# Four fused cross-attention layers: the third attention moved behind the next pair's first, value lanes spread by copies through memory, and an order of steps for each engine

## The chip, the cores and the metric

One core of one Trainium2 chip. The time is that of the whole launch on the device, in microseconds (us). The engines are TensorE (matrix products; PE in the profile, PEld for its weight loads), VectorE (DVE), ScalarE (ACT), GpSimd (POOL) and SyncE (SP), which here issues every DMA.

## What is computed

Sixteen sequences of 128 tokens and 256 channels pass through four layers, each with the same context `ctx`. All data is float32.

```python
# layer 0: 16 heads of 16; x attends to ctx and to itself; then RMSNorm and an MLP with GELU
# layer 1: 32 query heads, 8 key heads of 8; x attends to ctx; then LayerNorm
# layer 2: a recurrence over the tokens, 32 heads of 8, with the state from ctx
def step(s, inp):
    k_l, v_l, w_l, r_l = inp
    a = k_l[..., :, None] * v_l[..., None, :]
    out = jnp.einsum('bhs,bhst->bht', r_l, faaaa * a + s)
    s_new = a + w_l[..., None] * s
    return (s_new, out)
# r, k, v, g, w are projections of five mixtures of a token with the one before it;
# the result is normalised by head, gated by g, projected; then a gated feed-forward step
# layer 3: 16 heads of 16; x attends to LayerNorm(ctx); hidden + tanh(gate) * out @ Wo.T
```

## The kernel before

A **turn** works on a pair of sequences (`PAIR` = 2), so there are eight. A turn's work is cut into named **steps**, in three streams: entry (transposes `xT`, `cT` and the first queries, keys, values), front (layers 0 and 1, and layer 3's keys `k3` and values `v3`), and back (layers 2 and 3). Streams of different pairs run in one phase: `start` holds entry of pair 0; `first` front of 0 and entry of 1; each of six `steady` phases back of i, front of i+1, entry of i+2; `closing` back of 6 and front of 7; `last` back of 7.

**Order.** `SCHEDULE` is one hand-written list of steps for a steady phase. Every engine goes through the same list (`steps_of`) and does its own part of each step; each engine's queue is strict, and engines meet only at semaphores. `FIRST_ORDER` and `LAST_ORDER` serve the ends.

**Attention** runs in jobs (`("job", layer, n)`, 16, 16 and 8 a turn for layers 0, 1, 3). Job n multiplies scores for jobs n and n+1 (TensorE, line 534), masks them and finds the maximum (VectorE, L1020), exponentiates (ScalarE, L831), transposes (L548), copies out of PSUM (VectorE, L1035) and weighs values into the accumulator `psO` (L579, L587) with some steps' delay. `psO` is shared: attention 0, then the gathers of layer 2 (`y`), then attention 1, then attention 3 use it, each waiting until the one before is read.

**Products.** Other matrix results go through three PSUM banks (`ring`); a step's `start` waits until the product three before it has left. A product with two output tiles and two input tiles is 8 records of TensorE in the trace (L494, L504), a transpose step 4 (L485), m2 32 (L504 with hT).

**The lane steps** of layer 2 deal with the state s (8 by 8 a head) as 8 pairs u of lanes, with the token axis in the free dimension. For each u, `vr{u}` spreads v over the lanes by two products with a 0/1 matrix (`spread_v`, L599), VectorE multiplies the result in PSUM with k into `kv` (L1233), GpSimd puts the initial state in front (`seed`, L1381), VectorE runs two scans along the tokens (L1240) into `SS`, GpSimd multiplies by r into `Z` (L1371), and `gather` (odd v only, L614) sums lanes on TensorE into `psO`. `y` = psO + bonus (L1248). `kv` and `SS` are rings of two, `Z` of four. r is `rT`, v is `vT`, copied out of the product v2 at L1205; `ruk` is L1210, `g2` L1215, `bonus` L1220.

**Values.** `values16` (L1063, L1066) and `v1` (L1157) lay each value head beside zeros with 4 narrow instructions a product, so that 32-wide weight loads put a head in its rows.

`cT` is L1109, norms are L984 to L996, `o0` L1139, `m2` L1149, `o3` L1295. SP waits before each transfer for the reader of the old content; its order in a phase is mask and initial state of the back, mask 1, context, x and mask 0 of the entry, output.

## Time and profile before

| | |
|---|---|
| runs of the kernel before | 1258.09, 1263.58, 1264.42 us; median 1263.58 |
| profiled execution | 1264.44 us, of which span 1262.5 |
| TensorE (PE) busy | 1127.0 us, 89% |
| VectorE (DVE) | 956.6 us, 76% |
| ScalarE (ACT) | 651.5 us, 52% |
| GpSimd (POOL) | 261.0 us, 21% |
| mean granted TensorE clock | 0.945 of 2.4 GHz |
| moved by DMA | 18.91 MB, mean 15 GB/s |

The span runs from the first to the last instruction. Busy time of TensorE covers records whose ends are modelled; records of one kind overlap a little, so a group's busy time is less than count times mean. "Idle before" a group is time in which its engine stood still just before one of its instructions, with the engine that released it.

### The profile page before, as it was taken

To read this page: it belongs to the slowest core of one execution; us is meant where nothing else is said; L and a number is where in the kernel's file an instruction comes from. 1 tells how busy PE (TensorE), PEld (TensorE's weight loads), DVE (VectorE), ACT (ScalarE), POOL (GpSimd) and SP (SyncE) were. 2 spreads that over 40 slices of the span, in tenths; PEclk is the share of its full clock that TensorE was granted. 3 is DMA by queue.
4 is the path that set the end of the run, shared out by engine and by line. 5 is a ranking of instruction groups with operands and counts; after the bars stand their busy time and mean duration, and the time that the engine had idled before them with its cause. 6 is when DMAs were issued, how large, how long until landed. Compare 5 with 4: busy or idle time off the path is not lost. (4 is left out here: it accounts for less than half of the span.)

```text
span 1262.5 us, 24184 instructions
## 1 busy us (share of the span) xinstructions
PE 1127.0 (89%) x7776; PEld 765.1 (61%) x7776; DVE 956.6 (76%) x3401; ACT 651.5 (52%) x2483; POOL 261.0 (21%) x349
## 2 busy tenths in 40 slices
PE   5878899999999998999999998999999998897656
PEld 4564666665665666666666666666666666554434
DVE  2707697789967998789968998689968998675834
ACT  1528343784448553774448553674438553582024
POOL 3210223102410214102420214102321214101310
PEclk9788899999999999999999999999999999898858
DMA  8000000000000000000000000000000000000000
GB/s 296 2 9 20 1 2 1 22 2 15 2 21 2 16 1 1 22 2 16 1 22 2 12 5 1 22 2 15 1 22 2 6 11 1 1 2 11 1 1 9
DMA packets 18092, 18.91 MB, mean 15 GB/s; under 512 B 7216, under 2 KB 16432, under 8 KB 17712
## 3 DMA queue, kind: packets, MB, share of 16 engines
q1 hardware_dynamic: 17968, 17.37, 4.6%
q8 instruction: 64, 1.05, 0.3%
q14 instruction: 60, 0.49, 0.1%
HBM read 15.27 MB, written 2.10 MB: 14 GB/s over the span
## 5 line engine op out<-in xcount | busy, mean ns | idle before, releaser
L831 ACT ACTIVATE E<-S,nmax 128x128 f32<-128x128 f32 (+1 forms) x1024 | 424.1, 416 | 229.4 <-DVE nmax L1020 215.1
L1020 DVE CUSTOM_DVE_ANT_0 S<-psS,mb 128x128 f32<-128x128 f32 (+1 forms) x1024 | 264.3, 320 | 87.7 <-PE psS L534 64.4
L494 PE MATMUL ring<-slot,w_l 128*128 128x256 f32 x992 | 251.5, 400 | 14.0 <-DVE slot L1202 5.2
L494 PEld LDWEIGHTS ring<-slot,w_l 128*128 128x128 f32 x992 | 188.8, 198 | 60.0 <-issue 12.8
L548 PEld LDWEIGHTS psT<-ident,E 128*128 128x128 f32 x1280 | 146.2, 147 | 128.1 <-ACT E L831 73.3
L534 PE MATMUL psS<-keys,slot 32*128 32x512 f32 (+1 forms) x768 | 194.4, 581 | 30.1 <-DVE nmax L1020 19.0
L1035 DVE COPY ET<-psT 128x512 f32<-128x512 f32 x320 | 206.2, 681 | 7.8 <-PE psT L548 7.8
L548 PE MATMUL psT<-ident,E 128*128 128x128 f32 x1280 | 203.8, 293 | 7.8 <-DVE ET L1035 3.2
L831 ACT ACTIVATION_READ_ACCUMULATOR E<-S,nmax 128x1 f32 x1024 | 191.6, 187 | 0.0
L504 PE MATMUL ring<-w_l,slot 128*128 128x256 f32 (+1 forms) x640 | 151.9, 384 | 7.7 <-DVE slot L1051 5.8
L504 PEld LDWEIGHTS ring<-w_l,slot 128*128 128x128 f32 x640 | 115.3, 194 | 36.6 <-issue 10.7
L534 PEld LDWEIGHTS psS<-keys,slot 32*128 32x128 f32 x768 | 65.7, 190 | 78.6 <-DVE nmax L1020 37.7
L1240 DVE TENSOR_TENSOR_SCAN SS<-wP,kv 128x258 f32<-128x258 f32 x128 | 104.3, 854 | 2.2
L485 PE MATMUL ring<-ident,slot 128*128 128x128 f32 x384 | 61.0, 291 | 47.3 <-ACT slot L868 19.0
L1020 DVE DVE_READ_ACCUMULATOR2_ANT nmax<- 128x1 f32 x1024 | 84.7, 83 | 0.0
L485 PEld LDWEIGHTS ring<-ident,slot 128*128 128x128 f32 x384 | 46.3, 147 | 63.2 <-ACT slot L868 22.6
L1371 POOL TENSOR_TENSOR Z<-SS,slot 128x512 f32<-128x512 f32 x64 | 76.8, 1200 | 26.9 <-DVE SS L1240 26.9
L804 ACT ACTIVATE slot<-ring 128x512 f32<-128x512 f32 x72 | 42.5, 591 | 68.0 <-PE ring L485 55.3
L1389 POOL TENSOR_SCALAR veps<-mv 128x2 f32<-128x2 f32 x32 | 7.0, 218 | 314.0 <-DVE mv L989 314.0
L599 PE MATMUL ring<-slot,spread 128*128 128x256 f32 x256 | 70.2, 401 | 0.3
L815 ACT ACTIVATE hT<-ring,colt 128x256 f32<-128x256 f32 x64 | 26.9, 471 | 82.2 <-PE ring L494 82.2
L579 PE MATMUL psO<-ET,V 128*32 128x128 f32 x1536 | 63.2, 283 | 1.3 <-DVE ET L1035 1.3
(119 smaller groups left out, 1183.3 us busy)
## 6 DMA issues: line engine op xcount, KB each, us to landing
slot<-in_ctx SPq DMA_DIRECT2D x8, 256.0 KB, 2.7
slot<-in_x SPq DMA_DIRECT2D x8, 256.0 KB, 2.7
w_l<-in_wl SPq DMA_DIRECT2D x1, 2048.0 KB, 11.2
out<-slot SPq DMA_DIRECT2D x8, 256.0 KB, 2.1
w_l<-in_wl SPq DMA_DIRECT2D x2, 768.0 KB, 7.1
w_l<-in_wl SPq DMA_DIRECT2D x1, 1152.0 KB, 9.9
m0i<-in_m SPq DMA_DIRECT2D x8, 128.0 KB, 3.2
mb<-in_m SPq DMA_DIRECT2D x8, 128.0 KB, 2.8
```

What stands on the lines that cost most here:

```text
L485: m = pe.transpose(b[:, c, a * P:(a + 1) * P], src[:, a, c * P:(c + 1) * P], ident[:, :])
L494: m = pe.matmul(b[:, a, :], w[:, k, m0 + a * P:m0 + (a + 1) * P], src[:, k, :], start=(k == 0), stop=(k == kt - 1))
L504: m = pe.matmul(b[:, bb, 0:n], src[:, k, bb * P:(bb + 1) * P], w[:, k, :], start=(k == 0), stop=(k == kt - 1))
L534: ins = pe.matmul(psS[(first_job[layer] + m) % 2][:, x * w:(x + 1) * w], queries, keys[rows, group % RING_K, x * w:(x + 1) * w], start=Tru ...
L548: m = pe.transpose(psT[g % 2][:, k, :], E[:, g % RING_E, k * P:(k + 1) * P], ident[:, :])
L579: m = pe.matmul(psO[32 * c:32 * c + 32, t, bb * P:(bb + 1) * P], v[:, t * P + 32 * c:t * P + 32 * c + 32], e, start=(half == 0 and sblk == ...
L599: m = pe.matmul(b[:, a, :], spread_j[:, j + a, :], vT[:, ct, :], start=True, stop=True)
L831: ins = act.activation(E[:, g % RING_E, h * w:(h + 1) * w], S[:, g % RING_S, h * w:(h + 1) * w], ACT.Exp, bias=nmax[:, g % 4, h:h + 1], sc ...
L1020: ins = dve.tensor_tensor_reduce(S[:, g % RING_S, h * w:(h + 1) * w], psS[g % 2][:, h * w:(h + 1) * w], bias[:, bb, :], -1.0, HUGE, ALU.ad ...
L1035: dve.tensor_copy(ET[:, g % 4, :, :], psT[g % 2][:, :, :]).then_inc(sems["copied"], 1)
L1240: ins = dve.tensor_tensor_scan(SS[:, u % 2, a, :, :].rearrange("p b t -> p (b t)"), wP[:, ct, :, :].rearrange("p b t -> p (b t)"), kv[:, u ...
L1371: pool.tensor_tensor(Z[:, v % 4, :, :].rearrange("p a (b t) -> p a b t", b=PAIR), SS[:, v % 2, :, :, 0:P], r, ALU.mult).then_inc(sems["z"], 1)
```

## The change

Layer 3's attention (`job 3`, `inv3`, `sum3`, `o3`) becomes a fourth stream, one phase later: it now runs between attention 0 and the lane steps of the *next* pair, and `psO` is used in the order attention 0, attention 3, `y`, attention 1. `k3` and `v3` go from the front to the back stream. There are seven phases (`start`, `first`, `second`, five `steady`, `closing`, `last`, `end`), and the output and X4 get slots of their own (23, 24).

The spread products are gone. SP writes each half of `vT` to a buffer in memory, every row eight times, waits for each write, and reads it back in the lane layout, one transfer for each lane pair into a ring of four (`VR`). The multiplication with k moves from VectorE to GpSimd, which reads `VR`.

Values are written with one instruction a product; a weight load takes a `window` of 32 columns so that the head falls at its place.

Each engine has its own order (`PE_ORDER`, `ACT_ORDER`, `DVE_ORDER`, `POOL_ORDER`), written out for every phase; `@phase` names the phase of the words behind it, so that steps of two phases mix. In it `j3.6-7` are jobs 6 and 7 of layer 3. The quoted lines are one steady turn. Waits now count by these orders.

```diff
+def window(head, place, d):
+
+    at = 32 * head + 32 - d - d * place
+    return slice(at, at + 32)
...
+RING_V = 4
...
-SCHEDULE = [
-    "mask0", "xaT", *jobs(0, 0, 2), "shift1", *jobs(0, 2, 3), "cols", *jobs(0, 3, 4), "t", *jobs(0, 4, 8), "mw",
...
+PE_ORDER = """
...
+j1.8 v0l j1.9-11 o2 j1.12-13 k1 j1.14 xcT j1.15 @steady1 j0.0 @steady0 j1.16-17 fr j1.18 fk @steady1 j0.2 @steady0
+sum1 j1.19 @steady1 j0.3-4 @steady0 fv @steady1 j0.5-7 @steady0 o1 @steady1 j0.8-9 @steady0 x4T v1 @steady1 j0.10-11
+@steady0 q3 @steady1 j0.12-15 xaT j3.0 j0.16 k3 j0.17 j3.2 sum0 j3.3 j0.19 j3.4-5 o0 t j3.6-7 mw nT j3.8 mk mv j3.9 d1
+mr d2 v2 k2 j3.11 sum3 r2 o3 mg bonus u0 g2 u1 u2 u3 v3 gather1 m2 gather3 aT gather5 x1T q1 gather7 cT j1.0 yT xT
+j1.2 q0 j1.3 k0l ynT j1.4 k0c j1.5-7 v0c j1.8-9 v0l j1.10-11 o2 j1.12-13 k1 j1.14 xcT j1.15 @steady2 j0.0 @steady1
+j1.16-17 fr j1.18 fk @steady2 j0.2 @steady1 sum1 j1.19 @steady2 j0.3-4 @steady1 fv @steady2 j0.5-7 @steady1 o1
+@steady2 j0.8-9 @steady1 x4T v1 @steady2 j0.10-11 @steady1 q3 @steady2 j0.12-15 xaT j3.0 j0.16 k3 j0.17 j3.2 sum0 j3.3
+j0.19 j3.4-5 o0 t j3.6-7 mw nT j3.8 mk mv j3.9 d1 mr d2 v2 k2 j3.11 sum3 r2 o3 mg bonus u0 g2 u1 u2 u3 v3 gather1 m2
+gather3 aT gather5 x1T q1 gather7 cT j1.0 yT xT j1.2 q0 j1.3 k0l k0c j1.4 v0c j1.5-7 ynT j1.8 v0l j1.9-11 o2 j1.12-13
...
+ACT_ORDER = """
...
+@steady1 j0.3-9 @steady0 x4T @steady1 j0.10-11 @steady0 q3 @steady1 j0.12-15 xaT j3.0 k3 j3.1-2 sum0 j3.3-5 hn t
+apply0 j3.6-7 d1 d2 decay k2 sum3 r2 u0 g2 u1 u2 u3 aT x1T yT xT j1.0-1 yn k0l j1.2-4 ynT j1.5 k0c j1.6-13 k1 xcT
+j1.14-15 @steady2 j0.0-1 @steady1 fr fk @steady2 j0.2 @steady1 sum1 @steady2 j0.3-9 @steady1 x4T @steady2 j0.10-11
...
+DVE_ORDER = """
...
+cols j0.15 j3.0 j0.17 inv0 j3.2-3 shift1 sum0 j3.4-5 o0 j3.6-7 mw nT inv3 mk mv mr j3.9 v2 sum3 ruk o3 mg bonus vr0
+vr1 g2 vr2 vr3 v3 vr4 vr5 vr6 m2 vr7 q1 yT cT @steady2 norm3 @steady1 j1.0 @steady2 mask0 @steady1 yn j1.2-3 q0
+@steady2 apply3 @steady1 j1.4-5 y2 j1.6-7 v0c j1.8-9 v0l j1.10-11 o2 norm4 j1.12-13 apply4 j1.14-15 shift0 j1.17
+@steady2 j0.0 @steady1 inv1 @steady2 j0.2-3 @steady1 sum1 @steady2 j0.4-5 @steady1 fv @steady2 j0.6-7 @steady1 o1
...
+POOL_ORDER = """
...
+@steady0 norm1 @steady1 j0.12 @steady0 apply1 @steady1 sum0 @steady0 norm2 @steady1 j3.0 j3.4 hn j1.0 vr0 vr1 vr2
+gather0 vr3 gather1 vr4 gather2 vr5 gather3 vr6 gather4 vr7 gather5 gather6 gather7 x1T @steady2 norm3 @steady1 norm4
+@steady2 j0.0 j0.4 j0.8 @steady1 norm1 @steady2 j0.12 @steady1 apply1 @steady2 sum0 @steady1 norm2 @steady2 j3.0 j3.4
...
+FINAL = {"inv3", "sum3", "o3"}
...
+HAS = {"start": (0,), "first": (0, 1), "second": (0, 1, 2), "steady": (0, 1, 2, 3), "closing": (1, 2, 3), "last": (2, 3),
+       "end": (3,)}
+TIMES = {"start": 1, "first": 1, "second": 1, "steady": TURNS - 3, "closing": 1, "last": 1, "end": 1}
...
+IN_ORDER = {"start": [], "first": [0, 1], "second": [0, 1], "steady": [0, 3, 1], "closing": [0, 3, 1], "last": [3], "end": [3]}
...
-        spread_j = sb("spread", [8, P])
+        VR = sb("VR", [RING_V, 2, T])
+        v_rows = nc.dram_tensor("v_rows", (P, 8, CT * T), F32, kind="Internal").ap()
+        v_spread = v_rows.rearrange("(c a h) i n -> c a (h i) n", c=4, a=2)
...
+        slot = [sb(f"slot{n}", [512]) for n in range(1, 25)]
...
-        rT, X3, OUT = cm(18), tm(18), tm(18)
+        rT, X3, OUT = cm(18), tm(18), tm(23)
         kT, kk = cm(19), cm(19)
-        vT, tmpv, X4 = cm(20), tm(20), tm(20)
+        vT, tmpv, X4 = cm(20), tm(20), tm(24)
         gT, x4T = cm(21), cm(21)
         shifted = sb("shifted", [CT, PAIR, P + 1])
         wP = sb("wP", [CT, PAIR, P + 1])
...
+        V0 = sb("V0", [2, PAIR, 16 * 32 + 16])
+        V1 = sb("V1", [PAIR, 8 * 32 + 24])
+        V3 = sb("V3", [PAIR, 16 * 32 + 16])
...
+                final = {"steady": loop, "closing": TURNS - 3, "last": TURNS - 2, "end": TURNS - 1}.get(phase)
...
+                if back is not None:
+                    sp.wait_ge(leaves("v2"), left("v2"))
+                    for ct in range(CT):
+                        half = slice(ct * T, (ct + 1) * T)
+                        sp.dma_start(v_rows[:, :, half], vT[:, ct, :].unsqueeze(1).to_broadcast([P, 8, T]))\
+                            .then_inc(sems[f"v_out{ct}"], 16)
+                    for u in range(8):
+                        ct, j = u // 4, 2 * (u % 4)
+                        half = slice(ct * T, (ct + 1) * T)
+                        if j == 0:
+                            sp.wait_ge(sems[f"v_out{ct}"], turn(f"v_out{ct}"))
+                        if u >= RING_V:
+                            sp.wait_ge(sems["kv"], turn("kv", u - RING_V + 1))
+                        sp.dma_start(VR[:, u % RING_V, :, :],
+                                     v_spread[j % 4:j % 4 + 2, j // 4, :, half].rearrange("c p t -> p c t"))\
+                            .then_inc(sems[f"v_in{u % RING_V}"], 16)
+                if final is not None:
+                    sp.wait_ge(leaves("o3"), left("o3"))
+                    sp.dma_start(out[final], OUT).then_inc(sems["out_done"], 16)
+                if entry is not None:
                     if phase != "start":
                         sp.wait_ge(leaves("aT"), left("aT"))
-                    sp.dma_start(CX, ctx_in[shift:][entry]).then_inc(sems["c_in"], 16)
+                    sp.dma_start(CX, ctx_in[entry]).then_inc(sems["c_in"], 16)
...
-                        pe.wait_ge(sems["attn3"], before("attn3"))
+                        pe.wait_ge(sems["attn1"], before("attn1"))
+                    if layer == 3 and n == 0:
+                        if phase == "last":
+                            pe.wait_ge(sems["attn1"], before("attn1"))
+                        elif phase == "end":
+                            pe.wait_ge(sems["y"], before("y"))
+                        else:
+                            pe.wait_ge(sems["attn0"], turn("attn0"))
...
-                def spread_v(u):
-
-                    ct, j = u // 4, 2 * (u % 4)
-                    b = start(f"vr{u}")
-                    for a in range(2):
-                        m = pe.matmul(b[:, a, :], spread_j[:, j + a, :], vT[:, ct, :], start=True, stop=True)
-                    m.then_inc(sems["product"], 1)
...
-                    for half in range(2):
-                        for ct in range(CT):
-                            d = dst[:, :, half, ct * P:(ct + 1) * P]\
-                                .rearrange("p b (c h d) -> p b c h d", h=2, d=16)[:, :, :, half, :]
-                            at = ct * P + half * 64
-                            v = bank(phase, name)[:, :, at:at + 64].rearrange("p b (c d) -> p b c d", d=16)
-                            if name == "v3":
-                                ins = dve.tensor_copy(d, v)
-                            else:
-                                bias = row["v0_b"][:, at:at + 64].rearrange("p (c d) -> p c d", d=16)
-                                ins = dve.tensor_tensor(d, v, bias.unsqueeze(1).to_broadcast([P, PAIR, 4, 16]), ALU.add)
+                    d = dst[:, :, 16:].rearrange("p b (h x) -> p b h x", x=32)[:, :, :, 0:16]
+                    v = bank(phase, i, name).rearrange("p b (h d) -> p b h d", d=16)
+                    if name == "v3":
+                        ins = dve.tensor_copy(d, v)
+                    else:
+                        bias = row["v0_b"].rearrange("p (h d) -> p h d", d=16)
...
                             dve.wait_ge(sems["w"], turn("w"))
-                        dve.wait_ge(sems["product"], product(step))
-                        if u >= 2:
-                            dve.wait_ge(sems["scan"], turn("scan", u - 1))
                         dve.wait_ge(sems["seed"], turn("seed", u + 1))
-                        k_ = kT[:, ct, :].rearrange("p (b t) -> p b t", b=PAIR).unsqueeze(1)\
-                            .to_broadcast([P, 2, PAIR, P])
-                        dve.tensor_tensor(kv[:, u % 2, :, :, 1:P + 1],
-                                          bank(phase, step).rearrange("p a (b t) -> p a b t", b=PAIR), k_,
-                                          ALU.mult).then_inc(sems["emptied_D"], 1)
-                        dve.wait_ge(leaves(step), left(step))
...
+                        dve.wait_ge(sems["x4"], before("x4"))
+                        dve.wait_ge(sems["out_done"], before("out_done"))
...
+                def key_times_value(u):
+
+                    ct = u // 4
+                    pool.wait_ge(sems[f"v_in{u % RING_V}"], turn(f"v_in{u % RING_V}", 16 * (u // RING_V + 1)))
+                    k_ = kT[:, ct, :].rearrange("p (b t) -> p b t", b=PAIR).unsqueeze(1).to_broadcast([P, 2, PAIR, P])
+                    pool.tensor_tensor(kv[:, u % 2, :, :, 1:P + 1],
+                                       VR[:, u % RING_V, :, :].rearrange("p a (b t) -> p a b t", b=PAIR), k_,
+                                       ALU.mult).then_inc(sems["kv"], 1)
...
+                            pool.wait_ge(leaves("k2"), left("k2"))
                         seed(u)
+                        key_times_value(u)
...
```

## Rows read from the trace of the kernel before

**Rows 1.** Windows by phase. Columns: window, its length, busy us (records) of PE, PEld, DVE, ACT, POOL, PEclk, DMA share, GB/s

```profile
0.00:145.50 145.50, 115.92 (x696) 77.58 (x696) 70.75 (x310) 60.06 (x228) 26.96 (x42) 0.87 0.22 71
145.50:291.70 146.20, 138.79 (x978) 94.03 (x976) 118.90 (x425) 81.62 (x312) 31.61 (x41) 0.96 0.02 6
291.70:1008.50 716.80, 674.30 (x4862) 461.69 (x4860) 596.82 (x2116) 404.50 (x1551) 158.33 (x205) 0.99 0.03 9
1008.50:1149.70 141.20, 126.27 (x910) 83.61 (x908) 113.65 (x409) 77.90 (x304) 29.86 (x39) 0.96 0.02 4
1149.70:1262.50 112.80, 71.68 (x336) 48.17 (x336) 56.50 (x146) 27.43 (x91) 14.23 (x22) 0.72 0.02 6
```

**Rows 2.** Windows of one looped turn: v2's copy to `y`, and the rest

```profile
457.50:497.50 40.00, 36.09 (x264) 24.83 (x263) 37.86 (x77) 15.12 (x45) 16.13 (x22) 1.00 0.01 1
497.50:600.90 103.40, 98.81 (x712) 67.54 (x712) 81.68 (x348) 65.81 (x266) 15.47 (x20) 0.98 0.04 12
```

**Rows 3.** Windows of the last phase: to v2's copy, from there to `y`

```profile
1149.70:1173.10 23.40, 17.98 (x53) 11.07 (x54) 9.37 (x20) 3.22 (x8) 0.00 (x0) 0.64 0.06 14
1173.10:1199.40 26.30, 16.69 (x85) 10.82 (x83) 22.87 (x30) 1.80 (x4) 10.92 (x16) 0.88 0.00 1
```

**Rows 4.** Groups of TensorE: line, operation, shapes, count, busy us, mean ns, idle before

```profile
L599 PE MATMUL ring<-slot,spread 128*128 128x256 f32 x256 | 70.2, 401 | 0.3
...
L485 PE MATMUL ring<-ident,slot 128*128 128x128 f32 x384 | 61.0, 291 | 47.3 <-ACT slot L868 19.0 <-DMA slot<-in_ctx 10.2 <-DVE slot L996 7.4
L504 PE MATMUL ring<-w_l,hT 128*128 128x256 f32 x256 | 57.4, 382 | 1.2 <-ACT hT L815 0.9
...
L614 PE MATMUL psO<-Z,gather 128*32 128x256 f32 x256 | 21.5, 409 | 8.9 <-POOL Z L1371 8.9
```

**Rows 5.** TensorE in order of time: start, length, line, operation; a looped turn, last phase

```profile
452.62 3.72 PE L494 MATMUL ring<-slot,w_l 128*128 128x256 f32 x16 [0.74 <-DVE slot L1202]
...
457.28 1.13 PE L534 MATMUL psS<-keys,slot 32*128 32x512 f32 x4
458.34 1.09 PE L548 MATMUL psT<-ident,E 128*128 128x128 f32 x8
459.36 0.65 PE L579 MATMUL psO<-ET,V 128*32 128x128 f32 x16
...
1163.98 3.78 PE L494 MATMUL ring<-slot,w_l 128*128 128x256 f32 x8
```

**Rows 6.** Groups of VectorE: scans, key times value, one of the value copies

```profile
L1240 DVE TENSOR_TENSOR_SCAN SS<-wP,kv 128x258 f32<-128x258 f32 x128 | 104.3, 854 | 2.2
L1233 DVE TENSOR_TENSOR kv<-ring,slot 128x512 f32<-128x512 f32 x64 | 43.0, 672 | 4.1 <-PE ring L599 4.0
L1066 DVE TENSOR_TENSOR V<-ring,rowt 128x128 f32<-128x128 f32 x64 | 13.8, 279 | 13.7 <-PE ring L504 13.7
```

**Rows 7.** VectorE and GpSimd in order of time, two lane pairs of the last phase

```profile
1177.30 1.28 DVE L1240 TENSOR_TENSOR_SCAN SS<-wP,kv 128x258 f32<-128x258 f32 x2
...
1178.82 1.18 POOL L1371 TENSOR_TENSOR Z<-SS,slot 128x512 f32<-128x512 f32 x1
...
1181.21 0.21 POOL L1381 TENSOR_TENSOR kv<-s,wP 128x4 f32<-128x4 f32 x1 [1.21 <-DVE SS L1240]
1181.37 1.18 POOL L1371 TENSOR_TENSOR Z<-SS,slot 128x512 f32<-128x512 f32 x1
...
1181.75 1.93 DVE L1240 TENSOR_TENSOR_SCAN SS<-wP,kv 128x258 f32<-128x258 f32 x2
```

**Rows 8.** DMA: queue with packets, MB, share of 16 engines; issues with us to landing

```profile
q1 hardware_dynamic: 17968, 17.37, 4.6%
...
slot<-in_ctx SPq DMA_DIRECT2D x8, 256.0 KB, 2.7
...
w_l<-in_wl SPq DMA_DIRECT2D x1, 2048.0 KB, 11.2
out<-slot SPq DMA_DIRECT2D x8, 256.0 KB, 2.1
```

461 lines of the change are left out of this document (249 added, 212 removed).

## The prediction

> **What bounds the kernel now.** I read the busy time by phase first. Of the six looped turns the last five take 716.8 us, 143.4 each; there TensorE is busy 94% of the time (674.3 us), VectorE 83% and GpSimd 22% [rows 1]. The ends are looser: the last phase has TensorE busy 71.7 of 112.8 us at a mean clock of 0.72 [rows 1]. Next, one looped turn, from 457.5 to 600.9, cut at two places: the copy of v2 out of PSUM (457.5) and the end of `y`, the sum behind the last gather (497.5). Those 40.0 us hold 3.9 us of TensorE idleness, the other 103.4 us hold 4.6; VectorE has 2.1 us free in the 40.0, and 103.4 - 81.7 = 21.7 us outside [rows 2]. So TensorE's own work sets the length of a turn nearly everywhere, and the lane steps (vr0 to vr7 with the gathers) are the place where VectorE does. In the last phase the same steps take 26.3 us with VectorE busy 22.9 and TensorE only 16.7 [rows 3].
>
> **What the change takes away.** The eight spread products of a turn: 70.2 us of TensorE in the kernel [rows 4], 8.8 us a turn, so TensorE's busy time in a looped turn falls from 134.9 [rows 2] to 126.1. In the last phase TensorE is idle beside them, so there they give nothing. VectorE loses the key-times-value multiplication, 43.0 us, 5.4 a turn [rows 6]. The narrow value copies: 16 a turn at 0.22 us net (13.8/64) [rows 6] become three wide ones at the 0.67 of L1233 and one narrow, 3.5 to 2.2 us. VectorE's 119.5 us a turn become 112.8, less what its scans now wait for GpSimd (13.0 us a turn [rows 6] against eight pairs at 1.28 [rows 7]), so 110.0.
>
> **What it adds: the lane chain.** From v2's copy to `y` the path becomes: two writes of 1 MB to memory (each lane row eight times), a read of 256 KB per lane pair, then per pair a seed, the multiplication (now GpSimd), two scans (VectorE) and the Z product (GpSimd).
> The copies. 17,968 packets took 4.6% of 16 engines' span, 52 ns each [rows 8]. The writes are 2048 packets of 1 KB: 6.6 us. The first read is issued when the first write has landed, behind the second write in one queue: another 0.8 us for its 256 packets. A 256 KB write lands in 2.1 us and a read in 2.7 [rows 8], so some 1.9 us of a landing is not packets. 6.6 + 0.8 + 1.9, and 0.2 for issue: 9.5 us to the first multiplication. Bounds: 4.8 us (2.1 + 2.7, if size cost nothing) and 14 us (11.2, the landing of the 2 MB load, + 2.7) [rows 8]. I take 9.5, since packet time is the same everywhere in the trace. The other reads (0.8 us each) stay ahead of the steps.
> The steps. In the last phase Z starts at 1181.37 and takes 1.18 us; the scans start at 1181.75 and take 1.93 us, where two of them take 1.28 when alone [rows 7]: a scan waits for GpSimd to end. The mean scan takes 0.85 for the 0.64 of one alone [rows 6, 7]. The seed is 0.21 [rows 7]. Multiplication: not in the trace on GpSimd; Z has the same shape and number of inputs, 1.18. If one waits for the other throughout, a pair takes 0.21 + 1.18 + 1.18 + 1.28 = 3.85, less about 0.1 because a waiting scan ends a little sooner (1.93 against 0.80 + 1.28 = 2.08): 3.75, against 2.55 now (two Z starts at 1178.82 and 1181.37 [rows 7]). Bounds: 2.6 (GpSimd alone, nothing waits) and 3.9. Eight pairs: 30 us, 21 to 31.
> The Trainium skill's "SBUF — State Buffer", section "SBUF: two separate sides", says that GpSimd and a VectorE instruction with two SBUF inputs exclude each other for the whole instruction; the multiplication that this change moves had a PSUM input and was outside of that rule. By it alone a pair would be 3.89 and the sum 9 us longer than by the 3.75; the rows agree with it but for that 0.1.
> Chain from the end of v2 on TensorE to the end of the last gather: 0.7 (copy) + 9.5 + 30 + 0.65 (gather) + 0.4 of signals = 41.3 us.
>
> **What covers it.** In the new order of TensorE, from v2 to gather7 of a looped turn stand ten products of 8 records (k2, r2, o3, g2, u0 to u3, v3, q1) at 1.86 us (3.72/2 [rows 5]) = 18.6; m2 7.2 (57.4/8 [rows 4]); mg and bonus 1.0 each; sum3, aT, x1T 0.6 each (61.0 us for 96 [rows 4]); four gathers 2.7 (21.5/8 [rows 4]); one weighing step 0.65 [rows 5]. Sum 33. TensorE's queue is strict: it stands at gather5 and gather7, with layer 1's attention behind them, for 41.3 - 33 = 8.3 us, where it now loses 3.9.
> A looped turn: 41.3 + (126.1 - 33 = 93.1) + 4.6 (idle elsewhere, as now) = 139.0, 4.4 less than now. Five: -22.
> Second turn (now the first looped one, 146.2 [rows 1]): -8.8 spread; -13.3 for attention 3, which isn't there yet (four pairs of jobs at 2.7 us, from 457.28 to 459.98 [rows 5], = 10.8, sum3 0.6, o3 1.9); 34 us of cover, so 7 us of waiting for 3.9: +3. Together -19.
> Closing: -8.8, +4.4 for the wait, +13.3 for the attention 3 that comes from an earlier turn: +9.
> Last phase: the chain from v2's copy to `y` is 41.5 for 26.3 [rows 3]: +15. The attention of the turn before it (13.3) runs in front, where TensorE has idle 5.4 of 23.4 us at clock 0.64 [rows 3], and closing has 14.9 idle [rows 1]: I take 10 of the 13.3 as filled gaps (bounds 0 and 13.3): -10.
> First turn: k3 and v3 leave it (2 x 1.86, into the idle last phase): -4; its tail overlaps the next turn's jobs: TensorE is idle 29.6 us to 145.5 [rows 1], of which I take 4 (0 to 12).
> Small ones: the wait for the output's landing moves from ScalarE's r2 to VectorE's o3, a turn after that transfer: 0. SP's new waits (v2, then the ring of four) stand in front of the output and of the next CX and X. The ring is free some 26 us after v2, CX is wanted at cT, behind gather7 at 41; X waits for GpSimd's xb1, which stands behind the last Z, and comes near to when xT wants it: 0, at most 1 us a turn. The new slots and V tiles: 0.
> Sum against the profiled execution (span 1262.5, time 1264.4): 1264.4 - 22 - 19 + 9 + 15 - 10 - 4 - 4 = 1229.4, and the median of the runs is 0.9 below that execution. Forecast 1229.
>
> **Rivals.**
> (a) The chain is covered: scans and GpSimd run beside each other at 2.6 a pair, or the copies land in 5 us, or both in part. Then a looped turn is 126.1 + 4.6 = 130.7: five 41 us less than forecast, second 7, closing 8, last 9: 1164. For it: GpSimd is busy 31.7 of 143.4 us [rows 1]. Against it: the pattern of rows 7 repeats for every pair.
> (b) The clock. In the last phase, after waits, a product takes 3.78 us where it takes 1.86 in a looped turn [rows 5], and that stretch was granted 0.64 [rows 3]: the 1.2 GHz level for most of it. The looped turns are granted 0.99 [rows 1]; TensorE would now wait some 6 us at gather5 in each. Two products' worth at 1.2 GHz in seven turns: 2 x 1.9 x 7 = +27: 1256. The Trainium skill's "TensorE: Matmul & The Clock Gate", "Part 1: The HAM clock gate", says the same: throttled is the resting state and activity lifts it. Against: the wait at gather7 would absorb part of the slow stretch.
> (c) Slower: VectorE becomes the bound. It stands still in the chain for 41.3 - 17.6 us (16 scans 10.2, nine other steps 7.4), so 92.4 us of its work fall to the 97.7 us outside: 5 us of room where it has 21.7 now [rows 2]. Where its queue is in a stretch the later one (masks and copies of attention 1, token shifts, norms), TensorE waits for scores to be masked, and a turn is 146: +7 in seven turns, 1278. It decides once chain and VectorE's waits together cost 4.3 us a turn over the forecast (35 us over eight turns), that is, from a chain of 45.6 us, or copies of 14.
> (d) That the spread products were free already. In the 40.0 us they share TensorE is busy 36.1 [rows 2], so at most part of them; this lies inside (c).
>
> **How the numbers follow.** Forecast case 0.44 (own range 1205 to 1250), (a) 0.24 including halfway cases from 1160 to 1200, (b) 0.12, (c) 0.20. The range must leave out no more than 0.2: its low end 1172 cuts off about half of (a), its high end 1277 half of (c). A measurement of this kernel tells 0.5% (6.3 us) from no change. Faster by more: the forecast case, (a) and a third of (b): 0.70; within: 0.11; slower: 0.19.
>
> **What the changed profile would show.** TensorE busy near 1057 us and no line of spread products; GpSimd up by about 64 x 1.18 = 76 us, more if its records hold waiting. Looped turns of 139 us; TensorE's waits for Z grown from 8.9 us to some 50, in gather5 and gather7; scans with a mean well over 0.85 us; from v2's copy to the first multiplication 9 to 10 us; about 3.75 us from Z to Z; clock dips in every turn if (b). The prediction is wrong low if VectorE is busy or port-bound over 90% outside the chain, and wrong high if Z follows Z in 2.6 us.

## The result, and the profile after it

The changed kernel takes 1272.4 us (median of 17 runs, 1263.7 to 1281.9), the kernel before 1259.6 (17 runs beside them). The ratio of the runs is 1.0088, 95% interval 1.0058 to 1.0117 (that of the two medians is 1.010). Forecast were 1229 us, a range of 1172 to 1277 and, with 0.70, a faster kernel: the time lies near the upper end of the range, and the direction was wrong. The profiled execution of after is a long one: 1281.9 us, span 1280.0.

The page of after, the TensorE clock by fortieths of the span, and the groups that answer to [rows 4], [rows 6], [rows 7] and [rows 8]:

```profile
PE 1101.0 (86%) x7520; PEld 740.2 (58%) x7520; DVE 921.3 (72%) x3233; ACT 661.4 (52%) x2490; POOL 361.1 (28%) x413
...
PEclk9889796999999998999979999999999998689567
...
q1 hardware_dynamic: 52016, 50.93, 12.9%
...
L1326 DVE TENSOR_TENSOR_SCAN SS<-wP,kv 128x258 f32<-128x258 f32 x128 | 138.3, 1134 | 50.8 <-POOL Z L1463 44.1
...
L1481 POOL TENSOR_TENSOR kv<-VR,slot 128x512 f32<-128x512 f32 x64 | 92.1, 1440 | 20.5 <-DMA VR<-v_rows 20.5
...
L1463 POOL TENSOR_TENSOR Z<-SS,slot 128x512 f32<-128x512 f32 x64 | 85.6, 1339 | 15.0 <-DVE SS L1326 15.0
...
L723 PE MATMUL psO<-Z,gather 128*32 128x256 f32 x256 | 26.2, 496 | 50.2 <-POOL Z L1463 49.9
...
v_rows<-slot SPq DMA_DIRECT2D x16, 1024.0 KB, 6.5
VR<-v_rows SPq DMA_DIRECT2D x64, 256.0 KB, 3.7
```

TensorE waits 49.9 us for Z at the gathers (some 50 forecast, 8.9 before), the scans' mean is 1.13 us (forecast: well over 0.85). But TensorE is busy 1101 us where 1057 were forecast: the records are those expected, 256 fewer than before, and the granted clock is 0.917 for 0.945.

The windows of after, cut at the end of v2's copy of the first, the second, the seventh and the eighth turn (columns as in [rows 1]):

```profile
0.00:177.90 177.90, 148.94 (x981) 98.32 (x982) 102.07 (x391) 83.31 (x310) 34.52 (x52) 0.90 0.18 58
177.90:312.90 135.00, 121.16 (x826) 80.36 (x825) 106.59 (x375) 73.60 (x277) 42.52 (x46) 0.92 0.13 38
312.90:1042.20 729.30, 666.37 (x4752) 452.79 (x4751) 573.44 (x2034) 415.88 (x1577) 222.33 (x248) 0.96 0.12 38
1042.20:1174.50 132.30, 111.18 (x686) 72.52 (x685) 90.12 (x310) 64.41 (x247) 36.77 (x41) 0.86 0.12 35
1174.50:1280.00 105.50, 53.32 (x281) 36.17 (x279) 49.10 (x126) 24.19 (x82) 24.98 (x26) 0.69 0.15 45
```

The same cuts in the trace of before, and the cut used below for one of its turns (v2's copy to `y`, then the rest):

```profile
0.00:170.80 170.80, 138.81 (x840) 90.67 (x840) 91.09 (x379) 72.95 (x274) 29.97 (x46) 0.87 0.19 61
170.80:314.80 144.00, 136.47 (x974) 93.09 (x972) 119.62 (x423) 80.91 (x310) 31.62 (x41) 0.98 0.03 9
314.80:1031.40 716.60, 674.12 (x4862) 461.80 (x4860) 595.97 (x2115) 404.53 (x1550) 158.63 (x205) 0.99 0.03 9
1031.40:1173.80 142.40, 124.58 (x826) 83.00 (x825) 103.46 (x360) 68.90 (x266) 26.54 (x35) 0.92 0.01 3
1173.80:1262.50 88.70, 53.00 (x281) 36.50 (x279) 46.47 (x126) 24.21 (x83) 14.23 (x22) 0.74 0.01 4
```

```profile
458.20:496.80 38.60, 34.69 (x259) 24.13 (x258) 36.51 (x75) 14.64 (x44) 16.12 (x21) 1.00 0.01 1
496.80:601.60 104.80, 100.21 (x716) 68.22 (x716) 83.01 (x349) 66.28 (x267) 15.47 (x20) 0.98 0.04 12
```

Up to the second turn's v2 after is 1.9 us ahead (forecast 27), the five turns behind it cost 12.7 more (forecast 22 less), closing and end together 6.7 more (forecast 14). Against the forecast that is 25.1 us too long, 34.7 too long and 7.3 too short, 52.5 us in all.

One turn of after: v2's copy to `y`, and from there to the next v2's copy (columns as in [rows 2]; [rows 2] is the turn of before, with a cut at 457.5 that lies 0.7 ahead of the copy's end):

```profile
615.60:656.60 41.00, 34.20 (x177) 25.03 (x177) 24.91 (x30) 8.65 (x16) 25.06 (x25) 0.89 0.40 124
656.60:760.80 104.20, 97.97 (x742) 64.67 (x742) 86.46 (x368) 72.43 (x292) 19.71 (x24) 0.96 0.02 4
```

I call the first part the chain and the second the rest. In order of time, the chain of this turn:

```profile
624.94 1.27 POOL L1481 TENSOR_TENSOR kv<-VR,slot 128x512 f32<-128x512 f32 x1 [4.69 <-DMA VR<-v_rows]
...
629.28 1.70 POOL L1481 TENSOR_TENSOR kv<-VR,slot 128x512 f32<-128x512 f32 x1
...
630.94 1.18 POOL L1463 TENSOR_TENSOR Z<-SS,slot 128x512 f32<-128x512 f32 x1
...
633.46 1.57 POOL L1463 TENSOR_TENSOR Z<-SS,slot 128x512 f32<-128x512 f32 x1
...
648.74 1.08 PE L723 MATMUL psO<-Z,gather 128*32 128x256 f32 x8 [4.67 <-POOL Z L1463]
...
651.68 3.78 PE L612 MATMUL ring<-slot,w_l 128*128 128x256 f32 x8 [0.69 <-ACT slot L907]
```

And the granted clock around that gather (windows of TensorE alone: length, busy, PEclk, DMA share, GB/s):

```profile
644.00:646.00 2.00, 0.07 (x1) 1.00 0.00 0
646.00:648.00 2.00, 0.00 (x0) 0.89 0.44 131
648.00:650.00 2.00, 1.21 (x9) 0.50 0.00 0
...
654.00:656.00 2.00, 2.00 (x12) 0.50 0.33 101
656.00:658.00 2.00, 2.00 (x14) 0.55 0.30 95
658.00:660.00 2.00, 2.00 (x16) 1.00 0.00 0
```

The reader is to see three things. v2's copy ends at 615.6 and the first multiplication starts 9.4 us later: the copies are as forecast. The first Z starts 6.0 us behind that, after three multiplications. And gather5 waits 4.7 us, behind which the clock stands at 1.2 GHz for 9 us: a product of 8 records takes 3.78 us where it takes 1.86 at full clock [rows 5]. This is the mechanism of rival (b).

### The profile page after: what moved, and what is told of

Same layout as the page of the kernel before. It is cut to its first block, busy times and chain, and to the rows that moved or that the text cites. A ratio compares the mean times of both kernels' runs of the same rounds, so it can differ in the third digit from the quotient of the medians.

```text
span 1280.0 us, 23548 instructions
## 1 busy us (share of the span) xinstructions
PE 1101.0 (86%) x7520; PEld 740.2 (58%) x7520; DVE 921.3 (72%) x3233; ACT 661.4 (52%) x2490; POOL 361.1 (28%) x413
## 3 DMA queue, kind: packets, MB, share of 16 engines
q1 hardware_dynamic: 52016, 50.93, 12.9%
## 4 chain that ended last, share of the span: by engine, by line
PE 44%; DVE 14%; ACT 9%; POOL 7%; issue 6%; DMA 2%; DVEq 0%; POOLq 0%; ACTq 0%
PE ring L612 8%; PE ring L622 8%; PE psS L649 8%; PE psT L663 8%; ACT E L934 6%; DVE SS L1326 4%; POOL kv L1481 3%; PE ring L603 3%; POOL Z L1463 3%; PE psO L704 2%; DVE S L1114 2%; PE psO L696 2%; DVE ET L1129 2%; DMA VR<-v_rows 1%; DMA v_rows<-slot 1%
## 5 line engine op out<-in xcount | busy, mean ns | idle before, releaser
L612 PE MATMUL ring<-slot,w_l 128*128 128x256 f32 x992 | 259.6, 414 | 9.4 <-ACT slot L907 6.2
L612 PEld LDWEIGHTS ring<-slot,w_l 128*128 128x128 f32 x992 | 198.3, 207 | 55.0 <-issue 12.6
L1326 DVE TENSOR_TENSOR_SCAN SS<-wP,kv 128x258 f32<-128x258 f32 x128 | 138.3, 1134 | 50.8 <-POOL Z L1463 44.1
L622 PE MATMUL ring<-w_l,slot 128*128 128x256 f32 (+1 forms) x640 | 164.0, 405 | 9.0 <-DVE slot L1361 3.0
L622 PEld LDWEIGHTS ring<-w_l,slot 128*128 128x128 f32 x640 | 122.6, 207 | 37.5 <-issue 10.9
L603 PE MATMUL ring<-ident,slot 128*128 128x128 f32 x384 | 67.6, 307 | 40.0 <-DVE slot L1245 11.8
L1481 POOL TENSOR_TENSOR kv<-VR,slot 128x512 f32<-128x512 f32 x64 | 92.1, 1440 | 20.5 <-DMA VR<-v_rows 20.5
L1435 POOL TENSOR_TENSOR keys<-k0T,in 128x512 f32<-128x512 f32 x32 | 33.9, 1068 | 210.3 <-PE psS L649 205.0
L1463 POOL TENSOR_TENSOR Z<-SS,slot 128x512 f32<-128x512 f32 x64 | 85.6, 1339 | 15.0 <-DVE SS L1326 15.0
L603 PEld LDWEIGHTS ring<-ident,slot 128*128 128x128 f32 x384 | 47.4, 155 | 63.0 <-issue 23.1
L723 PE MATMUL psO<-Z,gather 128*32 128x256 f32 x256 | 26.2, 496 | 50.2 <-POOL Z L1463 49.9
```

The source lines that it names most:

```text
L603: m = pe.transpose(b[:, c, a * P:(a + 1) * P], src[:, a, c * P:(c + 1) * P], ident[:, :])
L612: m = pe.matmul(b[:, a, :], w[:, k, m0 + a * P:m0 + (a + 1) * P], src[:, k, :], start=(k == 0), stop=(k == kt - 1))
L622: m = pe.matmul(b[:, bb, 0:n], src[:, k, bb * P:(bb + 1) * P], w[:, k, :], start=(k == 0), stop=(k == kt - 1))
L1326: ins = dve.tensor_tensor_scan(SS[:, u % 2, a, :, :].rearrange("p b t -> p (b t)"), wP[:, ct, :, :].rearrange("p b t -> p (b t)"), kv[:, u ...
L1463: pool.tensor_tensor(Z[:, v % 4, :, :].rearrange("p a (b t) -> p a b t", b=PAIR), SS[:, v % 2, :, :, 0:P], r, ALU.mult).then_inc(sems["z"], 1)
L1481: pool.tensor_tensor(kv[:, u % 2, :, :, 1:P + 1], VR[:, u % RING_V, :, :].rearrange("p a (b t) -> p a b t", b=PAIR), k_, ALU.mult).then_in ...
```

## The experiments

A matmul of 128x256 counts as two records here, 0.465 us at full clock. Unless said otherwise a time is a median, measured beside the kernel before, whose median was 1258.8 to 1259.3 each time. One part of the change is in every kernel below and is nowhere tested alone: the values written with one instruction a product.

### Each half of the change alone

The third kernel puts the spread products back into the new orders:

```diff
-ORDER["POOL"] ... key_times_value(u)      (GpSimd, out of VR)
+ORDER["PE"] = with_spread(ORDER["PE"], ORDER["DVE"])   # vr0..vr7 as products of TensorE
+dve.tensor_tensor(kv[...], bank(phase, i, step), k_, ALU.mult)
```

> One part of the change alone: the new orders and the third attention behind the next turn's first, but the values spread by TensorE as before (eight spread products a turn, the key-times-value product on VectorE out of PSUM, no copies through memory; the spread products are put between the new order's products). By the terms of the forecast: second turn -13, closing +13, last phase -10, first turn -8: 18 us under the kernel before, 1242. TensorE busy near 1127 us and clock as before, 0.945. Rival (the new orders are what costs): 1265 or more, with TensorE's waits outside the lanes (E of ScalarE 25 us, nmax 19 us) as in the changed kernel.

It takes 1251.7 us, ratio 0.9955 (0.9927 to 0.9983), busy 1121 us, clock 0.957. The new orders are no cost; they are worth 7 us, less than half of the 18. TensorE's waits for E, 2.5 us before, are 23 here too.

The fourth does the reverse:

```diff
+PE_ORDER = ACT_ORDER = DVE_ORDER = POOL_ORDER = OLD_ORDER   # the schedule of the kernel before
-IN_ORDER = {..., "steady": [0, 3, 1], ...}
+IN_ORDER = {..., "steady": [3, 0, 1], ...}
```

> The other part alone: the values spread by copies through memory and the key-times-value product on GpSimd, but all four engines in the order of the kernel before, with the third attention in its old place. In that order v2 stands some 19 us ahead of vr0, so the 9.6 us of the copies are hidden; lane pairs come every 3.5 to 3.75 us where they came every 2.55. Theory: a looped turn loses 8.8 us of spread products and gains some 8 to 10 us of lanes with the 1.2 GHz stretch behind them, 143 to 147; the last phase is 10 to 15 us longer: 1270 to 1300. Rival (TensorE's 8.8 us a turn are the larger term, the lanes are hidden): 1215 to 1245.

1304.1 us, ratio 1.0349 (1.0322 to 1.0377), a looped turn 148.5. The copies and GpSimd's multiplication, alone, cost 45 us, though they take 70 us of work from TensorE. In the new orders the same exchange costs 21 us (1251.7 to 1272.4).

### Clock, copies and v2's place

The first kernel gives TensorE idle work in front of its waits:

```diff
+FILL = {"gather5": 16, "gather7": 8}
+pe.matmul(b[:, k // 2 % 2, :], W0["w1"][:, k % 2, 0:P], hT[:, k % 2, :], ...)   # n times, into the next bank
 gather_y(step[1])
```

> The changed kernel with idle work for TensorE: in front of gather5 16 matmuls and of gather7 8 matmuls (128x256, 0.23 us each at full clock) into the ring bank of the next product, which overwrites them; in the last phase 8, 24, 24 and 24 in front of the four gathers. Nothing else changes. Theory (the clock: the chain of lanes is as long as forecast, and what is lost to the forecast is TensorE at 1.2 GHz behind its waits at the gathers, busy time 1101 where 1057 was forecast): the 1.2 GHz stretches behind the gathers of the looped turns go, the looped turns shorten by 3 to 6 us each, the mean granted clock rises from 0.917 to over 0.94, and the time falls by 20 to 40 us, to 1235 to 1255. Rival (VectorE's and ScalarE's waits outside the chain set the turn): the clock rises all the same, the time stays within 5 us of the changed kernel's 1272. Second rival (the matmuls delay more than they give): slower than 1277.

1340.2 us. It was mis-sized: I had taken a matmul for one record, so 115 us were added, most of them longer than the wait. It only shows that the clock follows (0.943). The sized one:

```diff
+FILL = {("second", None, "gather3"): 6, ("steady", 1, "gather5"): 8, ("steady", 2, "gather5"): 8,
+        ("steady", 3, "x1T"): 8, ("steady", 4, "x1T"): 8, ("closing", None, "gather7"): 4, ("last", ...): 20, 12, 12, 6}
```

> The filling of the first experiment with its sizes mended: there a matmul counted as two records, so that 24 of them a turn took 11.2 us where 5.6 were meant, and the waits that they were to fill last 2 to 5 us. Now each stands in front of one wait of the changed kernel and is shorter than it (0.465 us a matmul): second turn gather3 6; first and second steady label after it gather5 8; third and fourth x1T 8; closing gather7 4; last phase 20, 12, 12 and 6 in front of the four gathers. Theory (clock): the 1.2 GHz stretches of 7 to 10 us behind each of these waits go; seven of them at some 4 us each and the last phase's 41 us, in which TensorE is busy a fourth of the time, 3 to 5 more: 1240 to 1255, clock over 0.935. Rival (what is late behind the wait is VectorE's or ScalarE's work and not TensorE's): clock up, time within 6 us of 1272.

1263.7 us, clock 0.940 in the profiled run and 0.940 to 0.959 in all: 9 us less than the changed kernel, under the 17 to 32 that I expected of the clock, over the rival's 6. The 1.2 GHz stretches are real. By the mean clocks, TensorE stands at that level for 152 us here and for 212 us in the changed kernel, and these 60 us are worth some 9.

```diff
-... mw mk mv ... d1 mr d2 v2 k2
+... mv mw mk v2 ... d1 mr d2 k2
```

> The changed kernel with v2 moved up in TensorE's and VectorE's order: mv is mixed before mw and mk, and v2 stands behind mk instead of behind d2. So the copies through memory start 3 to 6 us earlier, and nothing is added. Theory (clock and chain): the gathers' waits (49.9 us in all) fall to some 20, with them the 1.2 GHz stretches behind them; looped turns shorter by 4 to 8 us, 1225 to 1250. Rival (the wait moves: the chain then waits for k2 and the decay, or attention 3 is late for gather1, or the turn is set elsewhere): the gathers' waits fall but the time stays within 6 us of 1272.

1279.5 us (ratio 1.012, 1.006 to 1.018): no gain. From the `y` before it to v2's copy it is 109.1 us for 112.5 (up to the turn shown above), and in two later turns (the fifth looped and the closing one) the head start is lost again: GpSimd's first step waits for ScalarE's copies of k2 and r2, which didn't move, and the first multiplication comes 21.8 and 23.0 us behind v2's copy where it came 13.5 and 16.2. The rival held.

```diff
-sp.dma_start(v_rows[:, :, half], vT[:, ct, :].unsqueeze(1).to_broadcast([P, 8, T]))
+sp.dma_start(v_rows[:, half], vT[:, ct, :])
+... v_spread[j % 4 + c, j // 4, :, half].unsqueeze(1).to_broadcast([16, 8, T])
```

> The changed kernel with the values written to memory once (128 KB per half, not each row eight times, 1 MB) and read with the eightfold repetition in the read, two reads of 128 KB per lane pair. From v2's copy to the first multiplication 9.6 us become some 5.5 (no packet time of 1024 rows). Theory (the chain from v2 sets the turn wherever TensorE waits for Z or for m2's copy behind the scans): 3 to 4 us less in each of eight turns, 1240 to 1250. Rival (those waits are but a part, other waits take their place, as with the earlier v2): within 6 us of 1272.

1263.2 us: 9 less, a third of what was expected. The write lands in 1.8 us for 6.5 and the first multiplication comes at 5.0 for 9.4, but `y` at 37.6 for 41.0 only.

### Who multiplies

```diff
-pool.tensor_tensor(kv[...], VR[...], k_, ALU.mult)
+dve.tensor_tensor(kv[...], VR[...], k_, ALU.mult)
```

> The changed kernel with the key-times-value multiplication back on VectorE, its values now read from the copied rows in SBUF (two SBUF inputs); GpSimd keeps seed and Z. A pair takes 3.5 us now on average (31.5 us for eight with the last gather). Theory A (GpSimd's four steps in a row set the pair): without 1.26 to 1.7 us of GpSimd a pair takes 2.6 to 2.8, the lanes 22 to 24 us, and the time falls by 5 us a turn and more, to 1230 to 1245, although VectorE gets 43 us. Theory B (the two engines exclude each other whenever VectorE has two SBUF inputs, so that it doesn't matter which of them multiplies): a pair takes 0.2 + 0.7 + 1.3 + 1.2 = 3.4, the time stays within 8 us of 1272.

1241.0 us, ratio 0.9873 (0.984 to 0.9905): 31 us less than the changed kernel. But theory A is right in its time and wrong in its reason. The turn shown above, here (chain, rest; then two pairs in order of time):

```profile
609.70:645.60 35.90, 32.60 (x180) 24.84 (x179) 28.41 (x38) 8.64 (x16) 13.58 (x17) 0.95 0.42 132
645.60:748.40 102.80, 96.60 (x741) 64.17 (x740) 86.29 (x369) 72.16 (x292) 19.67 (x24) 0.97 0.03 7
```

```profile
626.08 1.28 DVE L1335 TENSOR_TENSOR_SCAN SS<-wP,kv 128x258 f32<-128x258 f32 x2
627.28 0.67 DVE L1328 TENSOR_TENSOR kv<-VR,slot 128x512 f32<-128x512 f32 x1
...
630.51 1.19 POOL L1472 TENSOR_TENSOR Z<-SS,slot 128x512 f32<-128x512 f32 x1
630.78 1.46 DVE L1328 TENSOR_TENSOR kv<-VR,slot 128x512 f32<-128x512 f32 x1
```

From the third multiplication to the seventh a pair takes 2.96 us, 3.42 in the changed kernel, between A and B. But from the first Z to the last it is 20.8 us in both, since the changed kernel has three multiplications done by its first Z; the gain shows at the two ends. The first Z comes 2.6 us behind the first multiplication, not 6.0, and the last gather ends 2.8 us behind the start of the last Z, not 4.8. `y` is at 35.9 for 41.0.

> Both of the last two edits together: values written once, multiplication on VectorE. If the length of the chain of lanes (copies and pairs) is what the changed kernel pays, the gains add up: by theory A some 9 us a turn of chain less, all waits of TensorE at the gathers gone, 1215 to 1235; by theory B 4 to 5 us less, 1240 to 1255. If the turn is set by TensorE's other waits and VectorE's load, 1262 or more.

This is the edit of e6 on top. 1244.4 us, ratio 0.9869 (0.9824 to 0.9913): nothing beyond e7. With the multiplication on VectorE its own queue (mg, o3, ruk, bonus) stands in front of the first pair in three of five turns, which starts 12 to 15 us behind v2's copy with either kind of write.

```diff
 FILL = ...      # on e7, sized to its waits: 8, 6, 8, 8, last phase 14, 8, 8, 6, 6, 6
```

> The multiplication on VectorE (as in the seventh experiment, 1241 us) and idle matmuls of TensorE in front of its waits: before the first scores of layer 1 in the second turn 8, before x1T of two turns 6 and 8, before q1 of the closing turn 8, and in the last phase 14, 8, 8 and 6 before the gathers, 6 before ynT and 6 before xcT, each shorter than the wait of that kernel that it fills (0.465 us a matmul). Theory (each wait over some 4 us costs 4 to 5 us again in the 1.2 GHz stretch behind it, as the sized filling of the changed kernel gave back 9): 1228 to 1236, clock over 0.945. Rival (nothing left of it once the lanes are shorter): 1238 to 1246.

1241.9 us, ratio 0.9836 (0.9793 to 0.988), clock 0.954. Against e7 (1241.0 us, ratio 0.9873) no gain shows beyond the noise, and the rival held.

```diff
-vr0 vr1 vr2 gather0 vr3 gather1 vr4 ...
+vr0 vr1 gather0 vr2 gather1 vr3 ...      # GpSimd's order, on the changed kernel
```

> The changed kernel with GpSimd's order changed alone: the Z product of pair u stands before the seed and the multiplication of pair u+2, not behind them. The first Z comes 1.5 to 1.9 us earlier. Theory (GpSimd is the engine that sets the lanes, busy or locked through all 31.5 us, so the order doesn't matter): the last Z and the time stay, 1265 to 1280. Rival (the two multiplications in front of the first Z are a cost of their own): the last gather comes 1.5 to 2 us earlier a turn, 1255 to 1264.

1268.6 us. The first Z comes 2.1 us sooner, the last 0.5 (35.6 for 36.1): Z now follows Z in 3.19 for 2.97. The median is 4 us under the changed kernel's, which its own spread of 18 us doesn't let me call a gain. GpSimd's order hardly matters; how much GpSimd has to do does.

### What TensorE's time is worth

```diff
 FILL = ...      # on e7: 16 matmuls a turn, in pairs, where e3 has its spread products
```

> The same multiplication on VectorE and copies through memory, and beside them 128 idle matmuls (16 a turn in pairs, 0.93 us a pair, some 60 us in all) at the places where the eight spread products of a turn stood in the third experiment. Nothing reads them; this is the price of the spread products' TensorE time alone. Theory (the cover forecast: TensorE's time is the bound in the looped turns, so it pays most of it): +35 to +55 us on 1241, 1276 to 1296. Rival (the spread products filled time in which TensorE would wait, and kept its clock up): within 12 us of 1241, clock 0.945 or more.

1250.1 us: 60 us of TensorE work inside the chain cost 9. Behind the first v2's copy e10 takes 1078.1 us and e7 1071.4, so the traces say 7. The kernel with the real spread products, e3, stands at 1251.7. So in the new orders, with the multiplication left on VectorE, putting copies in the place of the spread products is worth 11 us (e7 against e3), and the same TensorE work with nothing else changed 9. With idle work outside of the chain:

```diff
 FILL = ...      # on e7: 2 each before k0l, k0c, v0c, v0l, k1, fr, fk, q3 of six turns; closing 4 before fr, fk, q3
```

> The kernel of the seventh experiment (1241 us) with 108 idle matmuls outside of the chain of lanes: 2 in front of each of k0l, k0c, v0c, v0l, k1, fr, fk and q3 in the second to the last looped turn, 4 in front of fr, fk and q3 of the closing turn; 50 us in all, where the tenth experiment put 60 us inside the chain and paid 9. Theory (outside the chain TensorE's own work sets the turn): +40 to +50, 1281 to 1291. Rival (outside too something else sets it, VectorE's masks or ScalarE's exponentials): +5 to +20, 1246 to 1261.

1294.0 us: 50 us cost 53 (51 by the traces behind the first v2's copy). The same turn in both, chain and rest, first of e10, then of e13:

```profile
604.80:643.20 38.40, 37.71 (x212) 29.93 (x210) 28.16 (x38) 8.65 (x16) 14.37 (x17) 1.00 0.40 124
643.20:746.50 103.30, 97.11 (x741) 64.12 (x739) 86.29 (x368) 72.44 (x292) 19.68 (x24) 0.97 0.03 7
```

```profile
620.40:656.60 36.20, 32.78 (x180) 24.81 (x179) 28.42 (x38) 8.64 (x16) 13.59 (x17) 0.95 0.43 131
656.60:765.10 108.50, 103.52 (x772) 70.20 (x771) 86.45 (x369) 72.28 (x292) 19.78 (x24) 0.97 0.03 7
```

In e7 TensorE is busy 32.6 of the chain's 35.9. Thirty-two records more there fill the waits and leave the clock at 1.00; the chain grows by 2.5 us until TensorE fills it. In the rest, where TensorE is busy 96.6 of 102.8, 16 idle matmuls (7.4 us) cost 5.7 us in this turn; over the seven turns that have idle work the price is 4.8 to 10.0 a turn, 50.9 in all for 50.2.

The old order once more, with the multiplication on VectorE (the edits of e4 and e7):

> All four engines in the order of the kernel before, third attention in its old place, values spread by copies (hidden there: v2's copy stands 13 us ahead of the first multiplication), and the multiplication on VectorE. Against the kernel before only the spread products are gone from TensorE, and the multiplication reads SBUF. Theory (the multiplication on GpSimd is what made the fourth experiment 45 us slower): 1240 to 1258, near the kernel before or under it. Rival (the copies or the last phase's wait for them cost as much): 1275 or more.

```profile
452.70:494.30 41.60, 31.92 (x227) 21.39 (x225) 40.05 (x75) 14.57 (x44) 17.81 (x21) 0.88 0.34 108
494.30:597.90 103.60, 98.69 (x716) 67.42 (x716) 81.42 (x337) 66.33 (x267) 15.47 (x20) 1.00 0.04 10
```

1285.3 us, ratio 1.0184 (1.0144 to 1.0224). The work is that of the old turn [rows 2] but for the 32 records of spread (in the same cut before has 259 in the chain, here 227). TensorE now idles 9.7 us of the chain, the lanes take 3 us more (Z to Z 3.15 for 2.78), and a turn is 146.1 for 143.4 (the one shown 145.2). The theory (1240 to 1258) failed. With 8.8 us less of TensorE's work a turn follows the length of its lanes, and no gain shows. This run doesn't price the products by themselves, since the lanes became longer with them gone and the last part, from the last v2's copy, is 98.4 us for 88.7.

The last three cut work out of e7 instead, each from another engine.

```diff
+HALVED = {"q0", "k0l", "k0c", "v0c", "v0l", "fr", "fk", "q3"}
+kt = 1 if name in HALVED else w.shape[1]
```

> The same kernel with TensorE's work outside the chain cut: q0, k0l, k0c, v0c, v0l, fr, fk and q3 are computed from the first half of their input channels alone, 4 records in place of 8, some 60 us less in all (so these projections are not complete). Theory (TensorE sets the rest of the turn): 1241 - 45 to 60 = 1181 to 1196. Rival: another engine or the waits between the attention's steps set it, -5 to -20, 1221 to 1236.

1223.1 us (four runs, 1215.8 to 1241.9): 18 less for 60 us of work, as the rival had it. The turn shown gets 5.8 us shorter for 7.4 us of work, others 4.8, 3.6 and 3.6, and one gets 1.6 longer; over the kernel TensorE waits longer for masks (28.6 us for 18.0) and keeps its waits at the gathers. The granted clock is 0.918 here, 0.926 in e7's trace, so part of the saving may be lost to the clock; that is not shown.

```diff
+dve.tensor_copy(ET[:, g % 4, :, 0:n], psT[g % 2][:, :, 0:n])      # n = 64 behind the first turn
```

> The same kernel with VectorE's copy of the transposed exponentials cut to half its columns behind the first turn (0.68 us become some 0.4, 35 copies a turn, in all some 90 us less; the attention weighs with stale values in the other half). Theory (TensorE sets the rest of the turn): -5 to -20, from fewer waits for masks and copies: 1221 to 1236. Rival (VectorE at 84% is the bound there): -50 and more, under 1191.

1241.3 us: no difference, against the theory too, with VectorE busy 872 us for 949. VectorE's load is not what sets the turn of e7.

```diff
-accum_out=esum[layer][:, bb, at:at + 1])
+accum_out=esum[layer][:, bb, at:at + 1] if summed else None)
```

> The same kernel in which ScalarE's exponentials leave out their row sums behind the first ones (each has a read of the accumulator of 0.19 us behind it, 1024 of them; the attention is then normalised by old sums): some 165 us of ScalarE less. Theory: TensorE's waits for E (23 us) go, 15 to 25 us less, 1216 to 1226. Rival (these waits are replaced by waits for VectorE's masks in front of them): within 8 of 1241.

1230.5 us: 11 less with ScalarE busy 581 us for 661. Its row sums came to 80 us, half of what I had worked out. TensorE's waits for E fall from 23.1 to 13.0, about as much as the gain.

## Why the prediction was wrong

**The chain of lanes: right, by parts that were not.** 41.3 us were forecast; the five turns have 41.5, 41.2, 41.0, 41.9 and 44.4, mean 42.0. The copies' 9.5 us are 9.4 to 9.9 in four of them and 13.5 in the fifth; packet time was the right choice between the bounds (a packet took 51 ns on average, by 12.9% of 16 engines' span, for the 52 of the forecast). The multiplication, priced like Z at 1.18, takes 1.27 us alone and 1.44 on average. The lanes' 30.65 with the last gather are 31.5, but not as eight pairs of 3.75: multiplications follow each other in 3.4 and Z in 2.97, and two steps that the sum lacked make up for it, 6.0 us to the first Z and 4.8 from the last Z's start to the gather's end (with the multiplication on VectorE 3.4 and 2.0 of these are gone).

**The cover: right where it was counted.** 33 us were counted, for 180 records (ten products of 8, m2 32, gathers 32, the rest 36). In the turn shown the chain holds 177 records, and TensorE is busy 34.2 us in it, which includes the stretch at 1.2 GHz. The five turns aren't alike: the others hold 250, 178, 200 and 235 records there.

**The rest of the turn: this step failed.** "126.1 - 33 = 93.1, + 4.6" makes 97.7 us. Measured are 107.5, 112.5, 104.2, 94.7 and 100.5, mean 103.9. It is 103.5 in e7 and 103.2 in e3, and 104.8 in the kernel before with the same cut. So the sum said that 7 us of work, moved into the chain, shorten the rest by 7 us; they shortened it by 1. TensorE is busy there 97.6 us a turn for the 93.1, and idle 6.3 for 4.6. Parts of it can be named: the window holds 950 records a turn, where before has 972 with 32 of spread, so it took some work from the turns at its ends (the closing turn is 10 us shorter where I had 9 longer); the clock in the rest is 0.97 on average, 0.98 before, which is at most 1 us a turn; and the waits for E, 25 us for 2.5, are new with the orders, and halving them is worth 11 us (e16). Runs at either side fit a stretch held by TensorE and by its waits in turn: work added there costs 1.05 us per us (e13), work taken away gives 0.3 (e14), with longer waits for masks. How the 6 us a turn divide among these stays open.

**The spread products: nearly free, rival (d).** This is the same failed step seen from the other side. The forecast entered the change with -8.8 us a turn, and of its 1264 to 1229 it is the only large gain. I had the row that speaks against it: in the 40.0 us of the old chain TensorE is busy 36.1 [rows 2], and 27.3 without them. That stretch is as long as the lanes are, so their 8.8 us can only be gained if other work takes their place and the stretch that it came from gets shorter; the sum took that for granted (33 us of cover, 93.1 outside). I named this as (d), said that it "lies inside (c)", and gave it no chance and no time of its own. Measured: 60 us of such work are worth 9 (e10 against e7), and in the old order no gain shows (e12). As a time, worked out only now, (d) would have been, with the forecast's other terms: 1264.4, no gain from the products, the chain longer by 41.3 - 38.6 in seven turns (+19; 38.6 is the old chain in the cut used here), last phase +15 - 10, first turn -8: 1280. The profiled run is 1281.9, the median 1272.4. Rival (c) named 1278, as near, but by a mechanism that isn't there (below).

**GpSimd's multiplication.** It is the largest single price: 31 us (e7), and in the old order 19 (e12 against e4). The forecast had it in the chain's 41.3 and held it as covered up to 33. In the turn shown, 5.1 us less of chain gave 6.5 of the turn; the others give 6.1, 3.7, 0.3 and 0, closing 9.6, the last part 4.7.

**Rival (b), the clock: there, and overpriced.** The five looped turns have four waits of over 4 us (4.7, 4.7, 4.5 and 4.9), and TensorE's clock stands at 1.2 GHz for another 9.0, 9.1, 5.6 and 2.9 us from their ends; seven stretches of 3.4 us at that level lie elsewhere in them. 0.917 of 1280 us is 212 us at that level, where before it is 139. TensorE's busy time is 44 us over the forecast, which looks like the whole miss of 52.5 us in the profiled run (1280.0 against 1227.5). It isn't: filling the waits gives back 9 us of it, and no gain shows once the chain is shorter (e9). That the other slow records lie where something else was late in any case is what I conclude; no run isolates it.

**Rival (c), VectorE: no.** In the rest of the turn shown it is busy 86.5 of 104.2 us, where (c) had 92.4 of 97.7. Cut by 76 us in e7 it changes nothing (e15); the changed kernel itself wasn't tried so. Rival (a), 1164: no; the lanes weren't shorter.

**The ends.** To the second turn's v2 copy -27 were forecast, and -1.9 came, of which 8 us are this execution's own (below). Of the other 17, some 6 are the second turn's chain, whose last gather ends 47.4 us behind v2's copy for 41.3 (its Z follow each other in 3.71 us); the rest stays open. Last phase and closing: +14 forecast, +6.7 measured. (The chances that I counted as faster, 0.44, 0.24 and a third of 0.12, make 0.72, not 0.70.)

**VectorE and GpSimd in one pair of lanes.** GpSimd in the changed kernel, two pairs in order of time:

```profile
635.66 0.51 POOL L1473 TENSOR_TENSOR kv<-s,wP 128x4 f32<-128x4 f32 x1 [0.63 <-DVE SS L1326]
636.12 1.70 POOL L1481 TENSOR_TENSOR kv<-VR,slot 128x512 f32<-128x512 f32 x1
637.78 1.17 POOL L1463 TENSOR_TENSOR Z<-SS,slot 128x512 f32<-128x512 f32 x1
638.92 0.20 POOL L1473 TENSOR_TENSOR kv<-s,wP 128x4 f32<-128x4 f32 x1
639.07 1.26 POOL L1481 TENSOR_TENSOR kv<-VR,slot 128x512 f32<-128x512 f32 x1
640.30 1.56 POOL L1463 TENSOR_TENSOR Z<-SS,slot 128x512 f32<-128x512 f32 x1
```

These six steps take 6.4 us of the 6.83 to the next such seed, so GpSimd sets the pair, at 3.42 us for the 3.75 of the forecast. The multiplication takes 1.27 us alone (624.94) and 1.70 while a scan runs; on VectorE it takes 0.67, and 1.46 when it starts 0.27 us behind a Z of 1.19, so it ends 0.54 us after that Z. The Trainium skill's "SBUF — State Buffer", "SBUF: two separate sides", lets GpSimd and a VectorE instruction with two SBUF inputs exclude each other for the whole instruction; this trace agrees for the single instructions, and a pair of 3.89 by it was too long.

## What to carry to other kernels

Before work is taken from the busiest engine, cut the period at the places where that engine is not what is late, and price its work separately on both sides: here TensorE's added time cost 0.15 us per us inside the chain of lanes and about 1 outside, though it was busy over 90% on both sides. Put idle work there first; it is one edit and gives a price before anything is redesigned. It prices work added: work taken away outside the chain gave back only about a third. And a multiplication moved to an idle engine is dear when that engine stands in the chain: the version with it on VectorE, 1.3% faster than the kernel before, is the one to keep.

## What the runs showed of the chip

The first 981 TensorE records up to the first v2, the same instructions in the changed kernel and in e11, take 8 us more in one execution than in another, and TensorE's busy time in them differs by as much (148.9 and 140.7 us). The changed kernel has its first window above (177.9 us, clock 0.90); e11, whose edit lies behind this stretch, has:

```profile
0.00:170.00 170.00, 140.65 (x981) 93.27 (x982) 101.75 (x391) 83.19 (x310) 34.47 (x52) 0.95 0.19 61
```

Most of the 8 us comes at one place: a stretch at 1.2 GHz that begins at 125.3 us lasts 17.1 us in the first, and the one that begins at 124.1 lasts 3.4 in the second.

The 17 runs of the changed kernel spread over 18 us, and time and clock go together in them: 0.930 and 0.935 at 1263.7 and 1264.1 us, 0.917 to 0.919 at 1278 and over. In e7 they go together too: of six runs four are at 1240.3 to 1241.2 with a clock of 0.935 or 0.936, and two at 1248 and 1252 with 0.930 and 0.926. A low clock alone doesn't make a kernel's time unsure: e4, at 0.906 to 0.916, took 1303.1 to 1305.4 us in its four runs.
